# One transformer block on one core: V packed by pairs of tiles, value copies moved, norm work of qkv dealt to other slots

## The chip, the cores and the metric

One NeuronCore of a Trainium2 chip runs the program. The metric is device time in microseconds (us) of one execution, median of several runs; lower is better. The engines are TensorE (PE, with its weight loads shown apart as PEld), VectorE (DVE), ScalarE (ACT), GpSimd (POOL) and SyncE (SP, which issues the transfers). Each works through its own list of instructions in order, and semaphores tie the lists together.

## The reference

Input x is (2, 1024, 288), the condition (2, 288). First a conditional rotation, then one transformer block with 16 heads of 18:

```python
U, _ = jnp.linalg.qr(P)                      # 288 x 64
R = _rotation(cond, W, b)                    # expm of a skew matrix, 64 x 64
z = jnp.einsum('btn,nd->btd', x, U)
z_rot = jnp.einsum('btd,bde->bte', z, R)
x = x + jnp.einsum('btd,nd->btn', z_rot - z, U)
# block: ada = silu(c) @ ada_w + ada_b, split in shift, scale, gate (msa, mlp)
x = x + gate_msa * _attention(_modulate(_layernorm(x), shift_msa, scale_msa), ...)
x = x + gate_mlp * _mlp(_modulate(_layernorm(x), shift_mlp, scale_mlp), ...)
```

Attention is not over the sequence but inside each token: `attn = einsum('nthd,ntkd->nthk', q * scale, k)`, a 16 x 16 matrix of heads by heads for every token, softmax over k, then times v. The weights are large, so the kernel carries most operands as a high and a low float16 part.

## The kernel before

The 2048 tokens are 16 tiles (NT) of 128, in 4 chunks (NCH) of TPC = 4 tiles. A prologue computes the basis, the matrix exponential and the modulation (0 to 110 us). Then come qkv (120 to 207 us), attention (212 to 275 us), projection and the MLP.

**qkv.** It runs over slots `gu`. A unit (n, i, a, w) is one tile of chunk n and one of q, k, v (w = 0, 1, 2); twelve units (NQ) make a chunk. In each slot every engine goes through its own loop, written out by hand:
- TensorE: `turn` (a transpose block of the next chunk's normalised tokens) at the slots in TURN_AT, `qkv(gu)` (L819, seven matmuls of 288 columns; it waits for `low(gu - 2)`, since there are two banks UB), then the `job`s of the slot (L803 for q and k, L781 in `v_columns` for V: transposes of the finished q, k, v of a pair of tiles, two jobs a slot from slot 7), in some slots `maxima` (L768), and `delta` (L719, the rotation of a later tile) at the slots in DELTA_AT.
- ScalarE: `turn_out` (L1082, two results for each block of a turn), `high(gu)` (L1099, L1094: the float16 high part of a unit), `norm_root` (L1057, the square root for the layer norm of chunk 1 at slot 1, of chunk n + 2 at slot 8 of chunk n), and `job_out` (L1115, L1113: a cast of each job).
- VectorE: `split` (L1372, low part of a turn), `low(gu)` (L1418), `rotated` (L1384) and `stat` (L1318, L1320: statistics of a tile), `norm_var` (L1326), `norm_scales` (L1334 to L1342, five steps on 4 values a partition), `source` (L1351, normalises one tile an instruction, then L1356), and `maximum` (L1377).
- GpSimd: from the third unit on it folds the gate into the projection weights (L511 to L523).

The V half of a pair of tiles lies in HV as (slot, head, high/low, 18), with the two tiles (c_) in slots of their own. `v_columns` transposes each (head, tile) to 36 rows of a bank, tile 0 at partition 0 and tile 1 at partition 64 (R); `job_out` casts partitions 0 to 99 to VT. `v_groups` multiplies 36-row pieces of VT by SELV, which adds high and low part and puts tokens back on the partitions: bank VB[c_] holds tile c_, 16 groups of 18. `v_out` (L1150) copies both banks to VG for the values.

**Attention.** It is a loop over steps st. TensorE: `scores(st)` (L858), `maxima` of later steps, `values(st - 1)` (L895), late V transposes (`v_late`, L781, V of the second batch, four calls in steps 0 and 1 of each group of four from step 12), `turn_values` (L911) at step 2 of a group, `v_groups` (L881) at step 3. ScalarE: `exponentials` (L1141), `v_out`, and `values_out` (L1158), which copies four steps' values out of PSUM, up to step 16; from step DVE_AT = 17 VectorE does that copy (L1471), at steps 20, 24, 28, 32. VectorE also has `v_late_out` (L1475) and `normalise` (L1460, L1462). From step 11 on two pairs of score banks are used in turn (PAIRED = 10).

## Time and profile before

| | |
|---|---|
| time, median of 3 runs | 417.76 us (417.73 to 418.84) |
| the profiled execution | 418.09 us, of which the span from first to last instruction is 416.4 |
| busy: TensorE, its weight loads | 391.4 us (94%), 253.8 (61%) |
| busy: VectorE, ScalarE, GpSimd | 272.4 (65%), 228.0 (55%), 118.4 (28%) |
| granted TensorE clock, mean | 0.992 of full |
| chain that ended last | PE 72%, DVE 12%, ACT 10%, issue 6% |

The page names lines, engines and tiles; "L781 PE" is an instruction that line 781 issues on TensorE. Busy time of TensorE counts a matmul until its result has left the array, so neighbours overlap and a sum of durations is more than the time that they take. "Idle" times in square brackets tell how long the engine stood idle before a piece and what released it.

### The profile page before, as it was taken

The numbers are of one execution on the slowest core, as the hardware profiler recorded it, in microseconds if no ns is written. First come the engines' busy times: TensorE is split into PE (matmuls) and PEld (weight loads), VectorE is DVE, ScalarE is ACT, GpSimd is POOL, SyncE is SP. The second block draws the span as 40 slices with busy tenths as digits, with TensorE's granted clock in tenths as the row PEclk, the third lists the DMA queues.
The fourth block names the chain that finished last, engine by engine and source line by source line (L and its number), as shares of the span: only waits on it lengthen the run. The fifth ranks groups of instructions, "written<-read, shape, count | busy, mean of one in ns | idle before, by whom it ended". The sixth has DMA issues, their size and how long they took to land.

```text
span 416.4 us, 11776 instructions
## 1 busy us (share of the span) xinstructions
PE 391.4 (94%) x4799; PEld 253.8 (61%) x4799; DVE 272.4 (65%) x779; ACT 228.0 (55%) x478; POOL 118.4 (28%) x141
## 2 busy tenths in 40 slices
PE   8999999999988899999989788889999999999996
PEld 4665465666545566667656566568655575656575
DVE  2688885677689846655536256666899776756452
ACT  3356444432255799999876866656775432332200
POOL 6029999973009600010000000006500010101040
PEclk9999999999999999999979999999999999999999
DMA  5999100020000000000000000000000000000011
GB/s 163 298 318 270 50 4 2 2 74 2 2 0 2 2 2 3 2 3 6 2 6 6 3 3 3 2 3 2 1 2 1 16 28 16 30 14 30 14 45 43
DMA packets 8223, 15.30 MB, mean 37 GB/s; under 512 B 2591, under 2 KB 6279, under 8 KB 8044
## 3 DMA queue, kind: packets, MB, share of 16 engines
q1 hardware_dynamic: 8170, 14.56, 11.6%
q8 instruction: 38, 0.62, 0.6%
q14 instruction: 15, 0.12, 0.1%
HBM read 12.11 MB, written 2.38 MB: 35 GB/s over the span
## 4 chain that ended last, share of the span: by engine, by line
PE 72%; DVE 12%; ACT 10%; issue 6%; ACTq 0%; DVEq 0%
PE psum L972 13%; PE psum L988 13%; PE psum L541 9%; PE psum L819 5%; ACT scratch L1082 3%; PE psum L803 3%; PE psum L895 3%; ACT big L1115 3%; PE psum L633 2%; PE psum L949 2%; PE psum L645 2%; PE psum L597 2%; PE psum L624 2%; PE psum L911 2%; PE psum L637 1%
## 5 line engine op out<-in xcount | busy, mean ns | idle before, releaser
L972 PE MATMUL psum<-scratch,W 128*128 128x512 f16 (+1 forms) x252 | 57.9, 379 | 0.0
L988 PE MATMUL psum<-W,big 128*128 128x288 f16 x432 | 55.1, 286 | 0.0
L819 PE MATMUL psum<-WQ,scratch 128*128 128x288 f16 (+1 forms) x336 | 49.2, 287 | 4.5 <-DVE stage L1418 1.9
L1203 ACT ACTIVATE big<-psum 128x512 f32<-128x512 f32 x36 | 21.3, 597 | 57.3 <-PE psum L972 52.3
L988 PEld LDWEIGHTS psum<-W,big 128*128 128x128 f16 x432 | 42.2, 98 | 12.9
L541 PE MATMUL psum<-ident 128*32 128x192 f32 (+3 forms) x146 | 44.1, 386 | 0.0
L530 POOL TENSOR_TENSOR X<-X,big 128x288 f32<-128x288 f32 x16 | 13.0, 825 | 107.7 <-ACT big L1178 107.3
L1141 ACT ACTIVATE big<-psum 128x1024 f32<-128x1024 f32 x32 | 32.9, 1031 | 16.6 <-PE psum L858 16.3
L972 PEld LDWEIGHTS psum<-scratch,W 128*128 128x128 f16 (+1 forms) x252 | 24.7, 98 | 25.6
L819 PEld LDWEIGHTS psum<-WQ,scratch 128*128 128x128 f16 (+1 forms) x336 | 29.9, 98 | 15.4 <-DVE stage L1418 2.9
L1082 ACT ACTIVATE scratch<-psum,MOD 128x512 f32<-128x512 f32 (+3 forms) x48 | 34.4, 775 | 5.9 <-PE psum L744 4.6
L535 POOL TENSOR_TENSOR X<-X,scratch 128x288 f32<-128x288 f32 x16 | 13.5, 855 | 83.6 <-DVE big L1528 83.6
L1115 ACT CAST big<-psum 128x512 f16<-128x512 f32 x64 | 34.5, 599 | 0.1
L1041 ACT ACTIVATE scratch<-psum,scratch 64x65 f32<-64x65 f32 x63 | 19.5, 309 | 26.6 <-DVE scratch L1275 26.6
L1526 DVE TENSOR_SCALAR big<-big 128x512 f16<-128x512 f32 x36 | 15.6, 434 | 26.9 <-ACT big L1203 26.8
L1528 DVE SCALAR_TENSOR_TENSOR big<-big 128x512 f16<-128x512 f32 x36 | 26.3, 732 | 1.2
L1038 ACT ACTIVATE scratch<-scratch 64x1 f32<-64x1 f32 x63 | 12.8, 202 | 25.3 <-DVE scratch L1270 24.7
L1377 DVE TENSOR_REDUCE MX<-psum 128x16 f32<-128x1024 f32 x16 | 19.5, 1218 | 9.9 <-PE psum L768 9.9
L895 PE MATMUL psum<-big,scratch 128*32 128x128 f32 x512 | 23.1, 292 | 2.7 <-ACT scratch L1158 1.4
L1372 DVE TENSOR_TENSOR scratch<-scratch 128x512 f16<-128x512 f32 (+1 forms) x24 | 17.8, 740 | 11.3 <-ACT scratch L1082 11.1
L1099 ACT ACTIVATE stage<-psum 128x576 f16<-128x576 f32 x32 | 21.0, 655 | 7.0 <-PE psum L819 6.4
L803 PE MATMUL psum<-ident,stage 128*64 128x128 f16 x512 | 22.4, 223 | 2.4 <-ACT big L1115 1.4
(219 smaller groups left out, 758.3 us busy)
## 6 DMA issues: line engine op xcount, KB each, us to landing
X<-in_x_dram SPq DMA_DIRECT2D x4, 576.0 KB, 15.9
out_dram<-big SPq DMA_DIRECT2D x16, 144.0 KB, 1.7
big<-in_L_cond_W_dram SPq DMA_DIRECT2D x1, 2268.0 KB
big<-in_L_cond_ada_w_dram SPq DMA_DIRECT2D x2, 864.0 KB, 18.7
stage<-in_L_cond_fc_w_dram SPq DMA_DIRECT2D x1, 1296.0 KB, 19.4
big<-in_L_cond_fc_w_dram SPq DMA_DIRECT2D x1, 1152.0 KB
stage<-in_L_cond_qkv_w_dram SPq DMA_DIRECT2D x1, 864.0 KB
big<-in_L_cond_fc_w_dram SPq DMA_DIRECT2D x3, 144.0 KB
```

What stands on the lines that cost most here:

```text
L541: pe.matmul(out[:, 0:cols], left, left[:, 0:1].broadcast_to([P, cols]), start=True, stop=True)
L803: mm = pe.matmul(out[R * c_:R * c_ + R, P * hh:P * hh + P], HQ[:, 2 * (pr % 2) + c_, w, 4 * q + hh, :], ident16[:, :], start=True, stop=True)
L819: mm = pe.matmul(UB[gu % 2][:, 0:D], HT[0:r, n % 2, a_, P * a:P * a + P], WQ[0:r, w_, D * w:D * w + D], start=(p_ == 0), stop=(p_ == 6))
L895: mm = pe.matmul(PO[c_][32 * g:32 * g + 32, P * q:P * q + P], VG[:, w % 2, c_, 4 * q + g, :], E[:, s_ % 2, c_, P * g:P * g + P], start=Tru ...
L972: mm = pe.matmul(FB[idx % 3], W1[0:r, w_, P * m:P * m + P], HT[0:r, n % 2, a_, :], start=(p_ == 0), stop=(p_ == 6))
L988: mm = pe.matmul(YB[t % 2][:, 0:D], g[:, a_, f, cols], W2[:, w_, f, :], start=(f == 0 and a_ + w_ == 0), stop=(f == NF - 1 and w_ == 1))
L1082: act.activation(dst, src, ACT.Identity, scale=MOD[0:rows, 2 * l + 1, b, batch:batch + 1], bias=MOD[0:rows, 2 * l, b, batch:batch + 1]).th ...
L1099: act.mul(dst[:, :, 0:2, :] if w else dst[:, :, 0:3:2, :], src.unsqueeze(2).broadcast_to([P, H, 2, DH]), QSCALE / (FINE * FINE)).then_inc( ...
L1115: act.copy(columns(QKT[pr // 4][:, w, :], 16 * (pr % 4), q), src.rearrange("p (h v m) -> p h v m", h=4, v=32)).then_inc(col_done, 1)
L1141: act.activation(E[:, s_ % 2, :, :], psum[:, 3:5, :] if s_ > PAIRED and s_ % 2 else psum[:, 0:2, :], ACT.Exp, scale=DH ** -0.5 / (QSCALE * ...
L1203: act.activation(G32[:, idx % 2, :], FB[idx % 3], ACT.Gelu, scale=1.0 / (FINE * FINE)).then_inc(gelu_sb, 1)
L1528: dve.scalar_tensor_tensor(out=GT[c_ % 2][:, 1, m, :], in0=G32[:, idx % 2, :], scalar=FINE, in1=GT[c_ % 2][:, 0, m, :], op0=ALU.mult, op1= ...
```

## The change

- HV holds the two tiles of a pair side by side: (slot of pair, head, tile, high/low, 18). `v_columns` issues one matmul a head with 72 weight columns, where it issued two of 36; the result is 72 rows from partition 0. The casts on ScalarE and VectorE take partitions 0 to 71 instead of 0 to 99.
- SELV is 72 x 36 and its setup has two steps instead of four. `v_groups` issues 16 matmuls with 72 rows and 36 columns instead of 32 with 36 rows and 18 columns; a bank now holds 8 groups of both tiles, and `v_out` permutes while it copies.
- DVE_AT goes from 17 to 9: the value copies at steps 12 and 16 are VectorE's.
- In chunk 0 of qkv the turn for chunk 1 goes from slots 5, 6, 7 to 6, 8, 10 and the deltas from 4 to 7 to 5 to 8. On VectorE the last two statistics of chunk 1 are split over slots 0 and 1 (the first waits for one rotated tile less), `norm_var(1)` comes in slot 1, behind `low(1)`, `norm_scales(1)` goes from slot 1 to 3, its `source` from slots 2, 3 to 4, 5; ScalarE's `norm_root(1)` from slot 1 to 2.
- For chunks 2 and 3 `norm_root` goes from slot 8 to 9 of the chunk two before, `norm_scales` from 9 to 10; `source` stays at 10 and 11.

```diff
@@ -132,7 +132,7 @@
         BN = sb("BN", [P, 2, 6])
-        SELV = sb("SELV", [P, DH], F16)
+        SELV = sb("SELV", [P, 2 * DH], F16)
         ident16 = sb("ident16", [P, P], F16)
@@ -149,7 +149,7 @@
         o += 5 * CH
-        HV = scratch[:, o:o + 8 * D].bitcast(F16).rearrange("p (a h s d) -> p a h s d", a=8, h=H, s=2)
+        HV = scratch[:, o:o + 8 * D].bitcast(F16).rearrange("p (a h c s d) -> p a h c s d", a=4, h=H, c=2, s=2)
         assert o + 8 * D <= 4 * 2112 + 2 * D
@@ -269,8 +269,8 @@
         TURN1_AT = {2 * NCH: (3, 5, 7), 2 * NCH + 1: (5, 7, 8), 2 * NCH + 2: (3, 5, 7)}
-        TURN_AT = ((5, 6, 7), (2, 4, 6), (2, 4, 6), ())
-        DELTA_AT = ((4, 5, 6, 7), (1, 3, 5, 7))
+        TURN_AT = ((6, 8, 10), (2, 4, 6), (2, 4, 6), ())
+        DELTA_AT = ((5, 6, 7, 8), (1, 3, 5, 7))
         FC2_AT = (2, 4, 6, 8)
@@ -313,7 +313,7 @@
         PAIRED = 10
-        DVE_AT = 17
+        DVE_AT = 9
         EXP_TABLE_AT = 3 * NQ - 1
@@ -460,9 +460,9 @@
-            chain(pool.tensor_copy(SELV[:, :], ident[:, 0:DH]))
-            for j in (DH, R, R + DH):
-                chain(pool.tensor_tensor(SELV[:, :], SELV[:, :], ident[:, j:j + DH], ALU.add))
+            for c_ in range(2):
+                at = 2 * DH * c_
+                chain(pool.tensor_tensor(SELV[:, DH * c_:DH * c_ + DH], ident[:, at:at + DH], ident[:, at + DH:at + 2 * DH], ALU.add))
@@ -775,12 +775,10 @@
-                slot = 4 * (pr // 2 % 2) + 2 * (pr % 2)
                 for hh in range(4):
-                    for c_ in range(2):
-                        mm = pe.matmul(out[R * c_:R * c_ + 2 * DH, P * hh:P * hh + P],
-                                       HV[:, slot + c_, 4 * q + hh, :, :].rearrange("p s d -> p (s d)"), ident16[:, :],
-                                       start=True, stop=True)
+                    mm = pe.matmul(out[0:4 * DH, P * hh:P * hh + P],
+                                   HV[:, 2 * (pr // 2 % 2) + pr % 2, 4 * q + hh].rearrange("p c s d -> p (c s d)"), ident16[:, :],
+                                   start=True, stop=True)
                 return mm
@@ -875,11 +873,8 @@
                 for g in range(16):
-                    for c_ in range(2):
-                        r = R * c_
-                        at = P * (16 * (w % 4) + g)
-                        mm = pe.matmul(VB[c_][:, DH * g:DH * g + DH], VT[r:r + 2 * DH, at:at + P], SELV[r:r + 2 * DH, :],
-                                       start=True, stop=True)
+                    at, to = P * (16 * (w % 4) + g), 2 * DH * (g % 8)
+                    mm = pe.matmul(VB[g // 8][:, to:to + 2 * DH], VT[0:4 * DH, at:at + P], SELV[0:4 * DH, :], start=True, stop=True)
                 mm.then_inc(vg_psum, 1)
@@ -1091,7 +1086,7 @@
                         act.wait_ge(col_ready, JOB[(2 * (n - 2) + i // 2, 2, 3)] + 1)
-                    act.mul(HV[:, 4 * (n % 2) + i, :, 0, :], src, QSCALE / (FINE * FINE)).then_inc(qk_high, 1)
+                    act.mul(HV[:, 2 * (n % 2) + i // 2, :, i % 2, 0, :], src, QSCALE / (FINE * FINE)).then_inc(qk_high, 1)
                     return
@@ -1110,7 +1105,7 @@
                 if w == 2:
-                    act.copy(columns(VT, 16 * pr, q)[0:R + 2 * DH], src[0:R + 2 * DH, :].rearrange("p (h v m) -> p h v m", h=4, v=32)).then_inc(col_done, 1)
+                    act.copy(columns(VT, 16 * pr, q)[0:4 * DH], src[0:4 * DH, :].rearrange("p (h v m) -> p h v m", h=4, v=32)).then_inc(col_done, 1)
                 else:
@@ -1125,11 +1120,11 @@
                     high(gu)
-                if gu == 1:
+                if gu == 2:
                     norm_root(1)
                 for i in slots.get(gu, ()):
                     job_out(i)
-                if m == 2 * TPC and n + 2 < NCH:
+                if m == 2 * TPC + 1 and n + 2 < NCH:
                     norm_root(n + 2)
@@ -1146,8 +1141,9 @@
                     act.wait_ge(pv_ready, 4 * w - 4)
-                for c_ in range(2):
-                    cp = act.mul(VG[:, w % 2, c_, :, 0:DH], VB[c_][:, 0:16 * DH].rearrange("p (g d) -> p g d", g=16), 1.0 / QSCALE)
+                for v in range(2):
+                    cp = act.mul(VG[:, w % 2, :, 8 * v:8 * v + 8, 0:DH],
+                                 VB[v][:, 0:16 * DH].rearrange("p (g c d) -> p c g d", g=8, c=2), 1.0 / QSCALE)
                 cp.then_inc(vg_ready, 1)
@@ -1411,7 +1407,7 @@
                 if w == 2:
-                    hi, lo = HV[:, 4 * (n % 2) + i, :, 0, :], HV[:, 4 * (n % 2) + i, :, 1, :]
+                    hi, lo = HV[:, 2 * (n % 2) + i // 2, :, i % 2, 0, :], HV[:, 2 * (n % 2) + i // 2, :, i % 2, 1, :]
                 else:
@@ -1425,14 +1421,16 @@
                 if gu == 0:
+                    dve.wait_ge(x_rot, 2 * TPC - 1)
+                    stat(0, TPC + 2)
+                if gu == 1:
                     dve.wait_ge(x_rot, 2 * TPC)
-                    stat(0, TPC + 2)
                     stat(0, TPC + 3)
                     norm_var(1)
-                if gu == 1:
+                if gu == 3:
                     norm_scales(1)
-                if gu in (2, 3):
-                    source(1, 0, (range(0, 2), range(2, 4))[gu - 2])
+                if gu in (4, 5):
+                    source(1, 0, (range(0, 2), range(2, 4))[gu - 4])
                 if gu in AHEAD:
@@ -1440,7 +1438,7 @@
                         norm_var(n + 2)
-                    if m == 2 * TPC + 1:
+                    if m == 2 * TPC + 2:
                         norm_scales(n + 2)
@@ -1472,8 +1470,8 @@
                 dve.wait_ge(vcol_ready, 4 * (w - 4) + q + 1)
-                dve.tensor_copy(columns(VT, 16 * (w - 4), q)[0:R + 2 * DH],
-                                VB[q % 2][0:R + 2 * DH, :].rearrange("p (h v m) -> p h v m", h=4, v=32)).then_inc(vcol_done, 1)
+                dve.tensor_copy(columns(VT, 16 * (w - 4), q)[0:4 * DH],
+                                VB[q % 2][0:4 * DH, :].rearrange("p (h v m) -> p h v m", h=4, v=32)).then_inc(vcol_done, 1)
             for st in range(UNITS + 3):
                 for s_ in later(st):
```

## Rows read from the trace of the kernel before

**Rows 1.** The page, busy time, share of the span and instructions of TensorE
```profile
PE 391.4 (94%) x4799; PEld 253.8 (61%) x4799; DVE 272.4 (65%) x779; ACT 228.0 (55%) x478; POOL 118.4 (28%) x141
```

**Rows 2.** Busy time by stretch: us, PE, PEld, DVE, ACT, POOL busy; clock; DMA
```profile
120.00:144.20 24.20, 18.95 (x189) 11.94 (x190) 21.63 (x56) 15.31 (x30) 17.00 (x18) 1.00 0.00 1
144.20:167.30 23.10, 22.45 (x303) 15.18 (x302) 13.53 (x39) 22.05 (x44) 0.00 (x0) 1.00 0.01 3
...
212.30:220.30 8.00, 7.23 (x234) 5.11 (x236) 4.48 (x4) 4.53 (x6) 0.00 (x0) 0.57 0.03 7
...
235.60:243.40 7.80, 6.58 (x168) 4.56 (x168) 3.92 (x8) 5.56 (x9) 0.00 (x0) 1.00 0.01 2
```

**Rows 3.** Groups by line, TensorE: the V transposes; busy us, mean ns, idle before
```profile
L781 PE MATMUL psum<-ident,scratch 128*36 128x128 f16 x256 | 10.7, 221 | 1.5 <-DVE big L1475 0.9 <-ACT big L1115 0.4
```

**Rows 4.** The chain of waits in qkv: start us, us held, what
```profile
148.48 1.40 ACT scratch L1082 x2
...
154.25 0.54 ACT stage L1099
154.79 0.97 ACT big L1115 x2
...
165.83 0.97 PE psum L819 x7
166.80 0.56 PE psum L781 x16
...
197.54 1.83 PE psum L819 x14
```

**Rows 5.** Timeline of TensorE at step 11 of attention: start us, us, instruction
```profile
235.63 0.56 PE L881 MATMUL psum<-SELV,big 36*128 36x18 f16 x32 [0.25 <-DVE stage L1462]
236.03 0.40 PE L858 MATMUL psum<-big 63*128 63x128 f16 x8
236.36 0.64 PE L895 MATMUL psum<-big,scratch 128*32 128x128 f32 x16
```

**Rows 6.** Timeline of ScalarE: the V copies that close four groups of steps
```profile
236.22 0.72 ACT L1150 ACTIVATE scratch<-psum 128x288 f32<-128x288 f32 x2 [0.36 <-PE psum L881]
...
244.04 0.72 ACT L1150 ACTIVATE scratch<-psum 128x288 f32<-128x288 f32 x2 [0.36 <-PE psum L881]
...
251.85 0.71 ACT L1150 ACTIVATE scratch<-psum 128x288 f32<-128x288 f32 x2 [0.36 <-PE psum L881]
...
259.52 0.72 ACT L1150 ACTIVATE scratch<-psum 128x288 f32<-128x288 f32 x2 [0.35 <-PE psum L881]
```

**Rows 7.** Timeline of VectorE: norm steps and scalings in chunk 0 of qkv
```profile
124.03 0.17 DVE L1326 TENSOR_SCALAR ST<-MV 128x4 f32<-128x4 f32 x1
...
124.68 0.91 DVE L1336 TENSOR_TENSOR ST<-ST 128x4 f32<-128x4 f32 x1
...
126.95 1.72 DVE L1351 TENSOR_SCALAR scratch<-X,MV,ST 128x288 f32<-128x288 f32 x2
...
140.09 0.43 DVE L1326 TENSOR_SCALAR ST<-MV 128x4 f32<-128x4 f32 x1
```

**Rows 8.** Timeline of GpSimd: three of its 18 operations between 124.17 and 142.4
```profile
124.17 1.40 POOL L511 TENSOR_TENSOR big<-big 128x576 f32<-128x576 f32 x1 [13.59 <-PE psum L819]
...
126.40 1.28 POOL L513 TENSOR_TENSOR WP<-big,WP 128x576 f16<-128x576 f32 x1
...
131.14 1.41 POOL L511 TENSOR_TENSOR big<-big 128x576 f32<-128x576 f32 x1
```

**Rows 9.** Timeline of TensorE: the starts of units 4, 6 and 12
```profile
127.09 1.03 PE L819 MATMUL psum<-WQ,scratch 128*128 128x288 f16 x7 [1.45 <-DVE scratch L1418]
...
132.04 1.02 PE L819 MATMUL psum<-WQ,scratch 128*128 128x288 f16 x7
...
144.19 1.03 PE L819 MATMUL psum<-WQ,scratch 128*128 128x288 f16 x7
```

**Rows 10.** Who waited for whom, ScalarE, 120 to 144.2 us: in total, times, longest
```profile
ACT ST L1057 <- DVE ST L1326: 3.1, 2, 2.1
```

## The prediction

> **What bounds the kernel now.** The page comes first: TensorE is busy for 94% of the span [rows 1]. That share counts the pipeline's tail, so it doesn't say that TensorE sets every stage; the busy time in stretches does [rows 2]. In 120.0 to 144.2 us, where the first twelve units of qkv run, TensorE works 18.95 of 24.2 us, ScalarE 15.31, VectorE 21.63: nobody is full, the three wait for one another, and it is the one stretch of qkv that leaks. In 144.2 to 167.3 TensorE is at 97% and ScalarE at 95%, so a gain on one of them alone is mostly lost to the other. In attention (from 212.3) four score steps form a loop with a fixed period; in 235.6 to 243.4 TensorE has 6.58 of 7.8 us to do. The edits touch these three places and nothing else; prologue, projection and MLP stay.
>
> **Packed V: the transposes.** `v_columns` issues 256 matmuls of 128 columns in 32 calls of 8, 10.7 us of busy time [rows 3]. After, there are 128, each with 72 weight columns instead of 36. Counted by the mean that would be half. But look at the price of a column: in the chain of waits 7 qkv matmuls (288 columns, whole array) hold it for 0.97 us and 14 for 1.83 [rows 4], so 7 more cost 0.86, 0.123 each, 0.43 ns a column; one matmul of 128 columns alone costs 0.055. Sixteen transposes hold the chain for 0.56 us [rows 4], 0.035 each, which is less than a single one costs: the two of a pair run side by side in two column halves. Four packed ones cost what four pairs cost, 0.22 us. Nothing is saved here.
>
> What does change is what lies beside them. Seven qkv matmuls need 7 x 0.123 = 0.86 us, and hold the chain for 0.97 where transposes follow. Eight pairs need 0.44, and hold it for 0.56. So each change of the array's shape costs about 0.1 us. In the new form the transposes have the shape of qkv (72 columns don't fit a half), and both changes go. In qkv eight slots hold V jobs, hence 8 entries and 5 exits to a whole-array shape (four to qkv, one to a turn): at most 1.3 us. It counts only where TensorE is the later one. Two of the four slot pairs stand beside a turn, where ScalarE is behind; at the other two it idles 0.2 to 0.3 us a slot, so about 0.2 of each slot comes through. I take -0.4, ends 0 and -1.3. In attention the late transposes stand between the values (32 columns) and the row-tiled scores: both changes stay, 0.
>
> The Trainium skill, "TensorEngine Tiling (Array Packing)", Key Properties, says that changing the tiling mode drains the array; by that rule too the whole-array neighbours save a drain, and the rows agree. Its section The Solution promises up to 2x for sides of 64 or less when two tiles run at once, which speaks against fusing two tiles into one.
>
> **Packed V: the group sums.** `v_groups` issues 32 matmuls of 36 rows and 18 columns a call, in two row halves: from 235.63 to the scores at 236.03 it is 0.40 us, 0.025 for a pair [rows 5]. After: 16 of 72 rows and 36 columns on the whole array. By the column rate 36 columns are 0.015 us, under the present 0.025, so I keep 0.40. No row shows a 128-column weight load on the whole array with so short a matmul behind it; the bound above is that a matmul as wide as its load costs 0.055, so 16 would be 0.88, +0.48 us a call; the bound below is 0 (a call already pays 0.025 for a pair of loads). I take 0, the row nearest in shape. But the exit is new. Before, sums and scores have the same shape and follow with no gap, whereas from scores to values it is 0.33 us [rows 5] for 4 pairs at 0.055: 0.1 for the change of shape. That 0.1 now stands between sums and scores too. In the first three groups ScalarE hides it: its V copy of 0.72 [rows 6] lies ahead of the next exponential. From step 11 on, once VectorE owns the value copies, the loop is values, copy, late V copies, turn, normalise, sums, scores, values, and it lies on the path: 5 x 0.1 = +0.5.
>
> **Values by VectorE from unit 9.** The copies at steps 12 and 16 move. On ScalarE they lie between two exponentials. From V copy to V copy such a group takes 244.04 - 236.22 = 7.82 us; with the copy on VectorE 259.52 - 251.85 = 7.67 [rows 6]. Both kinds hold the same late V work, so the move is worth 2 x 0.15 = -0.3. VectorE has the room (3.92 of 7.8 us [rows 2]). Queued behind the copy on it are the late V copies, and the next turn waits for those; that wait is inside the 7.67. Attention together: +0.2, ends -0.3 and +0.7.
>
> **The norm work dealt anew.** This is the hard part, since GpSimd folds the projection weights from 124.17 on almost without a pause, and VectorE's operations from SBUF to SBUF wait for its current one. A step on 4 values took 0.17 us at 124.03, before GpSimd's start, and 0.91 at 124.68, ending at 125.59 with GpSimd's operation of 124.17 to 125.57; two row scalings took 1.72 [rows 7, 8]. Unblocked, two take 0.8. The Trainium skill, "SBUF — State Buffer", section "SBUF: two separate sides", says that the shared port pair is an exclusive lock held for a whole instruction; these ends agree.
>
> Before: the variance of chunk 1 is taken 0.14 us ahead of GpSimd's start; the scales follow at once, and unit 2's low half waits behind them, so that unit 4 starts at 127.09 [rows 9]. The scalings run from 126.95 [rows 7] to 129.9, then the first turn, unit 5 and a second turn; unit 6 starts at 132.04 [rows 9]. After, on VectorE:
> - low(1) goes ahead of the last statistics (0.6 us): unit 3 starts 0.7 earlier, at 123.9. The variance then falls at 124.4, inside GpSimd's first operation, and is held to 125.6, as the one at 140.09 took 0.43 [rows 7]. low(2) stands behind it: unit 4 at 126.05, 1.0 earlier.
> - The scales come after low(3), from 126.9. Two or three of their four lockable steps meet GpSimd's operations up to 129.0: they end at 128.5 to 129.05, and low(4) waits behind them.
> - Four scalings with low(5) between, each behind what GpSimd holds: the last one ends at 131.2 to 132.6. The first turn ends and unit 6 starts at 131.8 to 132.9. But before, a second turn (0.49) and one more delta (0.47) were done by unit 6.
> - From there ScalarE has three turns (1.40 each), five high halves (0.54), eight casts (0.97 a pair) [rows 4] and the root (0.2): 11.0 us, from about 132.3. Its longest wait for a root, 2.1 us [rows 10], shrinks to about 0.5, since that root is asked for a slot later, behind unit 9's casts. Unit 12's start follows the last of these casts by 0.3.
> Unit 12 comes out at 144.0 to 145.3 against 144.19 [rows 9]; I take 144.6, +0.4. With no port conflict the same chain puts the first turn at 129.4 and unit 12 at about 141.5.
> In chunk 1's turn for chunk 3 scales and scaling share a slot, 1.0 + 0.8 us ahead of the next low half, which the two qkv banks cover (TensorE has a slot of 1.5 us and the maxima in hand). 0, and +0.5 if that cover is gone. The SELV setup on GpSimd is two steps shorter, long before use: 0.
>
> **The sum.** Against the profiled execution (418.09 us: 416.4 of span and 1.7 around it): -0.4 for changes of shape, +0.2 for attention, +0.4 for the norm work: +0.2, 418.3. The median of the runs shown (417.76) is 0.33 lower: 418.0.
>
> **Rivals.**
> 1. The norm work wins: the steps slip through GpSimd's gaps, and ScalarE's 3.1 us of waits for roots [rows 10] vanish. Unit 12 at 141.5 to 143, -1.2 to -2.7; with the rest 414.9 to 416.4. For it: low(1) and low(2) are plainly freed. Against it: GpSimd's gaps are under 0.1 us. Chance 0.2.
> 2. Slower by the lock: the last scaling misses its gap and waits for GpSimd's 1.41 us from 131.14 [rows 8], the first split waits for the next one, the second root is late once more: unit 12 at 145.5 or later, +1.3 to +2, and no slack to bring in the changes of shape: 419.2 to 420. It decides from the point where the last scaling starts after 131.14. Chance 0.13.
> 3. Weight loads bound the group sums: +0.48 in seven calls on the path, +3.4: 421.4. Chance 0.05. The Trainium skill, "TensorE: Matmul & The Clock Gate", section "Weight-path perf modes", says that a load of 128 columns in 16 bits is fast whatever its rows, which speaks against it.
> 4. Halving by count: half of 10.7 us [rows 3], -5.3: 412.5. The side by side pairs stand against it. Chance 0.02.
> 5. The clock: around 212.3 to 220.3 it was 0.57 [rows 2], half speed for most of the group. It took 8.0 us without a turn of the values (1.1 us of TensorE), the later ones 7.8 with one, so the dip costs about 1.1. If the shifted work removes it: 416.9; a second dip: 419.1. Chance 0.05 each way.
>
> **How the numbers follow.** The likeliest (0.5, ends 416.9 to 419.0) gives 418.0. A measurement tells 0.3% (1.25 us) from no change: faster is under 416.5, slower over 419.0. Faster: most of rival 1, rival 4 and an edge of 5: 0.22. Slower: rivals 2 and 3: 0.18. Same: 0.60. The range takes in the near parts of rivals 1 and 2: 415.9 to 419.6.
>
> **What would show it.** Right: 128 transposes, four in what four pairs took; qkv before them holds the chain for 0.86 instead of 0.97; sums 0.40 us and scores 0.1 later; the group from step 12 at 7.75; the variance of chunk 1 at over 1 us instead of 0.17; the wait for the second root under 1 us; unit 12 at 144.6. Wrong: a variance that isn't held, a first turn before 130.5, sums over 0.5 us, or groups still at 7.8.

## The result and the profile after

Forecast was 418.0 us, 415.9 to 419.6, most likely no change. The changed kernel took 421.86 us in the median of 9 runs, against 418.33 for the kernel before on the same chip. Some executions of nearly every kernel fall into a slower state (here four of the nine, 432.8 to 436.8 us, and one of the nine before); ratios and the medians given from here on leave them out (421.31 against 418.15), and as the profiled executions of e1, e6, e7, e10, e11 and e13 are of that kind, with a prologue 12 to 49 us longer, their units are told from the start of unit 0 and their whole spans are not compared. The ratio is 1.0058, 95% interval 1.0033 to 1.0083: slower by 0.6%, about 2.4 us, and the time lies over the range's upper end. The profiled execution was 421.86 us with a span of 420.0, against 418.09 and 416.4, so the two traces differ by 3.6 us, and these 3.6 us are to be found. (The four other executions that count took 419.89 to 421.32, so the trace shows the longest of them.)

Line numbers moved up by two to five: qkv is L817, its turns' first transposes L744, V transposes L779, group sums L877, scores L856; on VectorE the low halves are L1414, variance L1322, scales L1330 to L1338, scalings L1347; on ScalarE roots are L1052.

Busy time by stretch in the changed kernel (columns as in [rows 2]):
```profile
120.00:144.20 24.20, 18.89 (x149) 11.45 (x149) 19.53 (x44) 12.36 (x23) 16.30 (x18) 0.86 0.00 1
...
238.85:246.60 7.75, 6.85 (x136) 4.70 (x137) 5.08 (x10) 4.71 (x7) 0.00 (x0) 1.00 0.01 2
```
The first row is the main finding. In the same 24.2 us TensorE was busy as long as before (18.89 against 18.95 us, [rows 2]) but got through 149 matmuls instead of 189, at a granted clock of 0.86 instead of 1.00. A busy share alone would have hidden it: the count beside it and the clock column show that the engine worked slower, not longer. The attention group, the last row, has 136 instructions where there were 168.

The starts answer to [rows 9]. TensorE in the changed kernel, from unit 2 to unit 12 of qkv:
```profile
123.07 1.96 PE L817 MATMUL psum<-WQ,scratch 128*128 128x288 f16 x14 [0.38 <-DVE stage L1414]
126.17 1.94 PE L817 MATMUL psum<-WQ,scratch 128*128 128x288 f16 x14 [1.15 <-DVE scratch L1414]
...
130.06 0.67 PE L744 MATMUL psum<-order,scratch 128*128 128x128 f32 x2 [1.48 <-DVE scratch L1347]
131.22 0.33 PE L744 MATMUL psum<-order,scratch 128*128 128x128 f32 x1 [0.49 <-DVE scratch L1347]
132.70 0.47 PE L744 MATMUL psum<-order,scratch 128*128 128x128 f32 x1 [1.15 <-DVE scratch L1347]
132.97 1.89 PE L817 MATMUL psum<-WQ,scratch 128*128 128x288 f16 x7
...
135.62 1.86 PE L817 MATMUL psum<-WQ,scratch 128*128 128x288 f16 x7
...
139.41 1.02 PE L817 MATMUL psum<-WQ,scratch 128*128 128x288 f16 x7
...
147.87 0.41 PE L817 MATMUL psum<-WQ,scratch 128*128 128x288 f16 x2
```
(The last row is cut by the view's end; unit 12 has its seven too.) Unit 6 starts at 132.97, unit 12 at 147.87, against 132.04 and 144.19. Units 6 and 7 take 1.89 and 1.86 us for the seven matmuls that take 1.02 before and after them. VectorE over the same stretch, to be read beside [rows 7]:
```profile
124.55 1.21 DVE L1322 TENSOR_SCALAR ST<-MV 128x4 f32<-128x4 f32 x1
...
127.14 0.69 DVE L1332 TENSOR_TENSOR ST<-ST 128x4 f32<-128x4 f32 x1
127.87 0.71 DVE L1334 TENSOR_TENSOR ST<-ST 128x4 f32<-128x4 f32 x1
...
129.49 0.86 DVE L1347 TENSOR_SCALAR scratch<-X,MV,ST 128x288 f32<-128x288 f32 x2
130.28 0.44 DVE L1414 SCALAR_TENSOR_TENSOR scratch<-psum,scratch 128x288 f16<-128x288 f32 x1
130.64 2.01 DVE L1347 TENSOR_SCALAR scratch<-X,MV,ST 128x288 f32<-128x288 f32 x2
```
and GpSimd's operations that these meet, as in [rows 8]:
```profile
124.33 1.40 POOL L511 TENSOR_TENSOR big<-big 128x576 f32<-128x576 f32 x1 [13.60 <-PE psum L817]
...
131.08 1.40 POOL L511 TENSOR_TENSOR big<-big 128x576 f32<-128x576 f32 x1
```
The variance of four values takes 1.21 us and ends with GpSimd's operation (125.73); the last pair of scalings takes 2.01 and ends at 132.65, behind the one that ends at 132.48. And the clock around that, from windows of the changed kernel:
```profile
128.60:132.70 4.10, 0.96 (x4) 0.42 (x4) 3.98 (x9) 0.00 (x0) 3.74 (x5) 0.88 0.02 4
131.70:138.50 6.80, 5.80 (x35) 3.21 (x36) 4.68 (x9) 3.08 (x5) 6.30 (x8) 0.50 0.00 0
220.50:223.90 3.40, 3.40 (x86) 2.34 (x82) 2.44 (x2) 1.05 (x2) 0.00 (x0) 0.50 0.02 5
```
In 4.1 us ahead of unit 6 TensorE worked 0.96: three transposes, and a fourth at 132.70 that unit 6 waits for. The clock fell at 131.7, inside this gap, to 0.50 (1.2 instead of 2.4 GHz), and stayed there for 6.8 us. Before, the dip stood in attention (213.3 to 220.1, [rows 2]); a shorter one is left there.

### The profile page after: what moved, and what is told of

It reads as the page before. It is cut to its first block, busy times and chain, and to the rows that moved or that the text cites. A ratio compares the mean times of both kernels' runs of the same rounds, so it can differ in the third digit from the quotient of the medians.

```text
span 420.0 us, 11263 instructions
## 1 busy us (share of the span) xinstructions
PE 393.2 (94%) x4543; PEld 255.6 (61%) x4543; DVE 275.5 (66%) x783; ACT 226.3 (54%) x474; POOL 117.1 (28%) x139
## 4 chain that ended last, share of the span: by engine, by line
PE 73%; DVE 11%; ACT 10%; issue 5%; POOL 1%; ACTq 0%; DVEq 0%
PE psum L967 13%; PE psum L983 13%; PE psum L541 8%; PE psum L817 5%; ACT scratch L1077 3%; PE psum L944 3%; PE psum L801 3%; PE psum L890 3%; ACT big L1110 3%; PE psum L633 2%; PE psum L645 2%; PE psum L597 2%; PE psum L624 2%; DVE scratch L1469 2%; PE psum L906 2%
## 5 line engine op out<-in xcount | busy, mean ns | idle before, releaser
L817 PE MATMUL psum<-WQ,scratch 128*128 128x288 f16 (+1 forms) x336 | 50.6, 294 | 2.5 <-DVE scratch L1414 1.2
L541 PE MATMUL psum<-ident 128*32 128x192 f32 (+3 forms) x146 | 44.1, 386 | 0.0
L817 PEld LDWEIGHTS psum<-WQ,scratch 128*128 128x128 f16 (+1 forms) x336 | 30.6, 100 | 14.0 <-DVE scratch L1414 1.7
## 6 DMA issues: line engine op xcount, KB each, us to landing
out_dram<-big SPq DMA_DIRECT2D x16, 144.0 KB, 1.7
big<-in_L_cond_fc_w_dram SPq DMA_DIRECT2D x3, 144.0 KB
```

The costliest lines, as they stand in the source:

```text
L541: pe.matmul(out[:, 0:cols], left, left[:, 0:1].broadcast_to([P, cols]), start=True, stop=True)
L817: mm = pe.matmul(UB[gu % 2][:, 0:D], HT[0:r, n % 2, a_, P * a:P * a + P], WQ[0:r, w_, D * w:D * w + D], start=(p_ == 0), stop=(p_ == 6))
```

## The experiments

Two theories at the start. **A**: the norm work loses by the port conflict with GpSimd's folding, and half clock follows. **B**: the loss comes from packed V or from the order of the norm work in itself. First each part alone.

**e1_pack and e11_pack_again: packed V alone** on the kernel before, with all hunks on `SELV`, `HV`, `VG` and the 72-row copies; the core of it:
```diff
-                    for c_ in range(2):
-                        mm = pe.matmul(out[R * c_:R * c_ + 2 * DH, P * hh:P * hh + P],
+                    mm = pe.matmul(out[0:4 * DH, P * hh:P * hh + P],
...
-                    for c_ in range(2):
-                        r = R * c_
+                    at, to = P * (16 * (w % 4) + g), 2 * DH * (g % 8)
```

> Only the packed V on top of the kernel before. My theory: it saves nothing by itself; changes of shape gain 0.1 to 0.4 us in qkv, and 0.1 us between group sums and scores costs up to 0.5 us in attention. Sum 417.5 to 418.5 against about 418.0 before, group period on VectorE's copies 7.74 instead of 7.67, unit 12 still at 144.2 us. Rival (the packing is what made the changed kernel slower): 420 or more.

> The packed V alone on the kernel before, once more, for a second profile and a tighter interval than 0.9948 to 1.0006. Theory (the two changes of array shape around each slot's V transposes go, sums to scores gains 0.09 us, and nothing else): 416.9 to 418.0, groups of four attention steps at 7.81 us with the values on ScalarE and 7.74 with them on VectorE, unit 12 within 0.3 us of +24.13. Rival (the gaps inside the bursts of small matmuls early in attention go too, since half as many instructions are issued): attention's first four groups together over 0.5 us shorter than in the kernel before, 416 to 417.

Measured: 0.9977 (0.9948 to 1.0006), and 0.9993 (0.9969 to 1.0016) the second time: no change that can be told. Relative to unit 0, unit 12 stands at +24.00 in e11 against +24.13. Its V copies, in attention:
```profile
255.97 0.71 ACT L1145 ACTIVATE scratch<-psum 128x288 f32<-128x288 f32 x2 [0.35 <-PE psum L877]
263.78 0.72 ACT L1145 ACTIVATE scratch<-psum 128x288 f32<-128x288 f32 x2 [0.35 <-PE psum L877]
271.52 0.72 ACT L1145 ACTIVATE scratch<-psum 128x288 f32<-128x288 f32 x2 [0.35 <-PE psum L877]
```
7.81 us with the values on ScalarE, 7.74 with them on VectorE, where [rows 6] has 7.82 and 7.67: the new shape change between sums and scores costs 0.07 where VectorE owns the values and nothing where ScalarE does. Its first attention group took 6.90 us with no half clock in it, against 8.00 in the kernel before with 6.8 us of half clock, so such a stretch costs 1.1 us there, as priced. e3, which is not packed and has no half clock in attention either, took 6.89, so packing has no part in that. The rival of the second text stays open. By its letter it came true, since the first four groups together are 1.0 us shorter than before; but the first group's clock makes all of that, and the next two take 8.00 and 7.45 us, against 7.90 and 7.45 in the kernel before, whose trace has no gap inside a burst of values.

e1's own trace shows something else: half clock for 6.8 us in chunk 0, from 8.7 us behind the start of unit 0, though the norm work is in its old order. Unit 6 came at +13.72 and unit 12 at +24.93, where e11, the same kernel, has +11.97 and +24.00.

**e2_dve: the values alone.**
```diff
-        DVE_AT = 17
+        DVE_AT = 9
```


> Only the value copies of steps 12 and 16 on VectorE. My theory: two groups go from 7.82 to 7.67 us, -0.3 us in all. Rival (VectorE's queue puts the late V copies behind and delays the turn): both groups at 8 us or more, +0.4 us.

Measured: 0.9993 (0.9975 to 1.0011), span 415.9. ScalarE's V copies in e2:
```profile
235.75 0.71 ACT L1150 ACTIVATE scratch<-psum 128x288 f32<-128x288 f32 x2 [0.35 <-PE psum L881]
243.43 0.71 ACT L1150 ACTIVATE scratch<-psum 128x288 f32<-128x288 f32 x2 [0.35 <-PE psum L881]
```
Both moved groups take 7.68 (the second ends at 251.10) instead of 7.82: -0.3 together, the forecast's term.

Its trace too has half clock in chunk 0, with the old order: 3.4 us from 127.2 on, where the 4.1 us ahead hold 1.98 us of work.
```profile
120.00:144.20 24.20, 20.07 (x191) 12.51 (x189) 21.49 (x55) 15.30 (x30) 16.98 (x18) 0.93 0.00 1
```
```profile
126.78 1.45 PE L819 MATMUL psum<-WQ,scratch 128*128 128x288 f16 x7 [1.45 <-DVE scratch L1418]
...
143.85 1.03 PE L819 MATMUL psum<-WQ,scratch 128*128 128x288 f16 x7
```
Unit 6 is 0.5 us late, but unit 12 starts at +24.10 from unit 0 (119.75), no later than before. So half clock in chunk 0 is not the new order's alone, and its price hangs on where it falls: nothing here, 0.9 us in e1, about 3 in the changed kernel (e9 below).

**e3_norm: the norm work alone**, with the hunk of e4 and the split of the statistics that e13 undoes (both below), chunk 1's root, scales and scalings in their new slots, and
```diff
-        TURN_AT = ((5, 6, 7), (2, 4, 6), (2, 4, 6), ())
-        DELTA_AT = ((4, 5, 6, 7), (1, 3, 5, 7))
+        TURN_AT = ((6, 8, 10), (2, 4, 6), (2, 4, 6), ())
+        DELTA_AT = ((5, 6, 7, 8), (1, 3, 5, 7))
```

> Only the norm work dealt anew. My theory: all of the loss is here, +2 to +3.7 us over the kernel before (420 to 421.7): the first turn ends after 132.5 us, TensorE idles over 3 us before it and its clock falls to half for 6.8 us there; unit 12 at 146.5 to 148 us. Rival (the loss needs the packing too): under 419.5.

Measured: 1.0060 (1.0031 to 1.0089), span 420.0, the changed kernel's ratio and span. Unit 6 starts at 132.89, unit 12 at 147.88. Windows of e3 ahead of unit 6 and behind it:
```profile
128.50:132.60 4.10, 0.97 (x4) 0.42 (x3) 3.96 (x9) 0.00 (x0) 3.71 (x5) 0.88 0.01 4
131.60:138.40 6.80, 5.78 (x35) 3.19 (x36) 4.67 (x9) 3.06 (x5) 6.31 (x8) 0.50 0.00 0
```
The whole loss, with its gap and its dip, is the norm work's: packed V (0.9977 and 0.9993) and the values (0.9993) show none of it alone.

**e4_roots: of that, only the later roots and scales of chunks 2 and 3.**
```diff
-                if m == 2 * TPC and n + 2 < NCH:
+                if m == 2 * TPC + 1 and n + 2 < NCH:
                     norm_root(n + 2)
...
-                    if m == 2 * TPC + 1:
+                    if m == 2 * TPC + 2:
                         norm_scales(n + 2)
```


> Of the norm work only the second part: root and scales of chunks 2 and 3 one slot later, chunk 1 as before. My theory: ScalarE's wait of 2.1 us for the root at 138.4 to 140.6 us shrinks to under 1 us and unit 12 starts 0.3 to 1.3 us earlier than 144.2: 416.7 to 417.7. Rival (scales and scaling in one slot put the next low half late): 418 or more, unit 12 or 13 not earlier.

Measured: 1.0003 (0.9979 to 1.0026). Unit 12 starts at 143.14, 0.9 earlier from unit 0 than before, and the first scores 1.0 earlier (210.53). But attention's first two groups give it back: 8.12 and 8.66 us instead of 8.00 and 7.90. TensorE in the second of them:
```profile
223.01 0.64 PE L895 MATMUL psum<-big,scratch 128*32 128x128 f32 x14 [0.19 <-issue]
...
227.71 0.42 PE L895 MATMUL psum<-big,scratch 128*32 128x128 f32 x7 [0.46 <-issue]
```
The gaps lie inside a burst of values whose operands are there, and the profile names no releaser. The traces of e3, e10 and e12, not packed either, have one such gap each, 0.42, 0.17 and 0.46 us; those of the kernel before, of e2 and of the packed kernels have none. What makes them stays open, and whether packing removes them too. The time, 417.88 in the median, shows no gain, though the forecast was 416.7 to 417.7.

**e5_fold_late: the changed kernel, folding later.** The one-line edit starts GpSimd's folding behind unit 14 instead of unit 2.
```diff
-            pool.wait_ge(qk_ready, 3)
+            pool.wait_ge(qk_ready, 15)
```


> The changed kernel, with GpSimd's folding of the projection weights started after unit 14 instead of unit 2, so that nothing holds VectorE in chunk 0. Theory A (the port makes the turn late): variance of chunk 1 back at 0.17 us, first turn ends at 129 to 130 us, no half clock there, unit 12 at 141.5 to 143 us instead of 147.9; the run 415 to 418 us, so 3 us or more of the loss is gone. Theory B (the new order itself is late, whatever GpSimd does): unit 12 at 146 us or later, 420 or more.

Measured: 0.9946 (0.9926 to 0.9966), a median of 416.56 us, where the changed kernel has 1.0058: 1.1%, or nearly 5 us, less. VectorE, the same steps as above:
```profile
125.48 0.17 DVE L1322 TENSOR_SCALAR ST<-MV 128x4 f32<-128x4 f32 x1
...
127.25 0.16 DVE L1332 TENSOR_TENSOR ST<-ST 128x4 f32<-128x4 f32 x1
...
129.46 0.76 DVE L1347 TENSOR_SCALAR scratch<-X,MV,ST 128x288 f32<-128x288 f32 x2
```
0.17 instead of 1.21, 0.16 instead of 0.69, 0.76 instead of 2.01. Unit 6 stands at +9.29 from unit 0 (121.15) instead of +12.75, unit 12 at +21.11 instead of +27.65, with the clock at 1.00. Theory A stands: without the lock there is neither the late turn nor the half clock. Attention took two half-clock stretches of 3.4 us each.

**e6_warm and e9_warm8: the gap filled.** The changed kernel with 12, then 8, calls into an idle bank ahead of chunk 1's first turn, two instructions each; what they compute is read by nobody.
```diff
+                        if gu == 6:
+                            for _ in range(8):
+                                clock(CB[0], ident[:, :], 2 * P)
```


> The changed kernel with 12 idle matmuls (0.32 us each, 3.8 us) on TensorE ahead of chunk 1's first turn, into a bank that nobody uses yet. The wait for the turn stays, only the clock can differ. Theory A1 (the half clock behind the wait costs about 2.5 us of the 3.6): no half clock at 131 to 139 us, unit 6 still at 132.9, unit 12 at 145 to 145.5 instead of 147.9, 418 to 419.5 us. Theory A2 (the wait alone is the loss, the clock costs under 0.5 us): unit 12 at 147.4 or later, 420.5 or more.

> The changed kernel with 8 extra matmuls into an idle bank on TensorE, in the gap ahead of chunk 1's first turn (12 in the run before, where they overshot the gap by about 1.3 us). At full clock 8 take about 1.7 us, at half clock 3.4. Theory (TensorE's idle stretch of about 4.3 us costs the clock, and the half clock costs 3.0 us between units 6 and 12): unit 6 stays at about +12.75 us from unit 0's start, no half clock follows it, and unit 12 comes at +24.6 to +25.2 instead of +27.65; the time is 418.3 to 419.5, that is 2 to 3 us under the changed kernel. If the busy stretch is too short and the clock falls all the same, unit 12 stays at +27.6 and the time at 421 to 422. Rival (the loss sits in the order, not in the clock): unit 12 at +27 or later whatever the clock does, 421 or more.

Measured, e6: 1.0043 (1.0018 to 1.0067), a median of 419.68 us, just over the forecast; 12 were too many, unit 6 came 1.3 us late, at +14.06, but with the clock at 1.00 it took 11.89 us from unit 6 to 12 instead of 14.90. e9: 1.0042 (0.9999 to 1.0084); of the seven times that the comparison rests on five are 417.3 to 418.64 and two 422.42 and 423.51, hence the wide interval. No trace shows what those two met. Its profiled execution is one of the five, with a span of 416.8:
```profile
120.00:144.20 24.20, 21.48 (x193) 14.60 (x194) 20.65 (x50) 14.96 (x29) 16.35 (x18) 1.00 0.01 1
131.70:138.50 6.80, 6.69 (x73) 4.28 (x72) 5.82 (x13) 5.43 (x10) 6.31 (x8) 1.00 0.00 0
212.90:219.80 6.90, 6.11 (x193) 4.36 (x196) 3.74 (x4) 3.62 (x6) 0.00 (x0) 0.51 0.02 6
```
```profile
128.20 3.75 PE L541 MATMUL psum<-ident 128*128 128x256 f32 x16
...
132.56 1.02 PE L817 MATMUL psum<-WQ,scratch 128*128 128x288 f16 x7
...
144.38 1.02 PE L817 MATMUL psum<-WQ,scratch 128*128 128x288 f16 x7
```
The idle work (L541; 3.75 us at full clock, not the 1.7 expected) fills the gap, the clock stays at 1.00 through 131.7 to 138.5, where 73 instructions pass instead of 35. Nothing on VectorE or GpSimd changed; the last scalings still take 2.01 us. Unit 12 stands at +24.47 from unit 0 (119.91): 3.2 us less than the +27.65 of the changed kernel, and 0.3 more than the kernel before. So of the 3.5 us by which unit 12 is late, 3.2 are clock and 0.3 all the rest, the later turn among it. In the time the same holds only for those five executions.

**e7_pack_dve_roots and e8_pdr_fold: the change without chunk 1's new slots**, then with the line of e5 too. Against the changed kernel e7 has the statistics of e13 (below) and
```diff
-        TURN_AT = ((6, 8, 10), (2, 4, 6), (2, 4, 6), ())
-        DELTA_AT = ((5, 6, 7, 8), (1, 3, 5, 7))
+        TURN_AT = ((5, 6, 7), (2, 4, 6), (2, 4, 6), ())
+        DELTA_AT = ((4, 5, 6, 7), (1, 3, 5, 7))
...
-                if gu == 2:
+                if gu == 1:
                     norm_root(1)
...
-                if gu == 3:
+                if gu == 1:
                     norm_scales(1)
-                if gu in (4, 5):
-                    source(1, 0, (range(0, 2), range(2, 4))[gu - 4])
+                if gu in (2, 3):
+                    source(1, 0, (range(0, 2), range(2, 4))[gu - 2])
```

> The changed kernel with chunk 1's norm work, turn and deltas put back to their old slots; packing, value copies, and the later roots of chunks 2 and 3 stay. If the parts add: roots -0.9 us at unit 12, packing -0.5 to -1.0, copies -0.3: 416 to 417 us. If the gains are given back in the first two groups of attention (as with the roots alone): 417.5 to 418.5. No gaps of 0.4 us or more inside TensorE's bursts in 211 to 236 us, where the unpacked kernels have them at full clock.

> As the one with chunk 1's work put back, and GpSimd's folding started after unit 14. Theory A: chunk 0's steps are no longer held (0.91 back to 0.2, 1.72 back to 0.8), first turn ends at about 128.5 instead of 130.1 us, unit 12 at 141 to 142 us: 414.5 to 416 us, unless the folding now holds VectorE and with it ScalarE in 147 to 165 us, which would give 1 us or more back (unit 24 no earlier than 166).

Measured, e7: 0.9979 (0.9955 to 1.0002), unit 12 at +23.15, 0.85 us earlier than in e11. Its first two groups of attention took 7.88 and 7.97 us, so they don't give the gain back as in e4, and there is no gap inside a burst, as expected. Yet the ratio can't be told from those of packed V alone, so the roots' gain isn't shown in the time. e8: 0.9926 (0.9903 to 0.9949), 415.17 us, unit 12 at +19.81. Against e5, which has chunk 1's new slots and no conflict either, that is 1.3 us earlier: at unit 12 the new order of chunk 1's norm work is worse also with no lock in it. (The two ratios' intervals overlap.)

**e12_fold_only: the kernel before with the folding late.**
```diff
-            pool.wait_ge(qk_ready, 3)
+            pool.wait_ge(qk_ready, 15)
```

> The kernel before with GpSimd's weight folding started after unit 14 instead of unit 2, and nothing else. Theory (the port conflict is what chunk 0 of qkv leaks): unit 6 at +9.5 to +10.5 us from unit 0 instead of +11.98, unit 12 at +20.5 to +21.5 instead of +24.13, and 415 to 416.5, some of the 3 us given back early in attention; and then packed V, VectorE's values and the later roots are worth 0.3 to 1.3 us more (the kernel with all four took 415.18). Rival (the gain of 3 us came mainly from the later roots and packed V, with late folding only helping them): unit 12 at +22.5 or later and 417 or more.

Measured: 0.9912 (0.9890 to 0.9935), a median of 414.13 us from only three executions, and a span of 412.7. Starts of units 0 and 12 on TensorE (a query that ended at 140.9 cuts the second):
```profile
120.45 0.91 PE L819 MATMUL psum<-WQ,scratch 128*128 128x288 f16 x6 [0.53 <-DVE scratch L1372]
...
140.75 0.42 PE L819 MATMUL psum<-WQ,scratch 128*128 128x288 f16 x2
```
Unit 12 at +20.30 instead of +24.13. And the folding costs nothing where it went; e12's stretch of units 12 to 24:
```profile
140.70:163.80 23.10, 22.46 (x306) 15.17 (x300) 14.75 (x37) 22.05 (x45) 16.52 (x18) 1.00 0.01 3
```
It is the row 144.20:167.30 of [rows 2] with 16.5 us of GpSimd added: as long, TensorE 22.46 against 22.45, ScalarE the same; VectorE's busy time grew by the 1.2 us in which it was held, and it has 8 us to spare.

**e10_split_rows: the kernel before with the two statistics split**, the second one and the variance behind low(1).
```diff
                 if gu == 0:
+                    dve.wait_ge(x_rot, 2 * TPC - 1)
+                    stat(0, TPC + 2)
+                if gu == 1:
                     dve.wait_ge(x_rot, 2 * TPC)
-                    stat(0, TPC + 2)
                     stat(0, TPC + 3)
                     norm_var(1)
-                if gu == 1:
                     norm_scales(1)
```


> The kernel before with one thing moved on VectorE: of chunk 1's two last statistics, the second, with the variance behind it, goes behind low(1); square root, scales, scalings, turns and deltas stay in the kernel before's slots. Theory (the variance of 4 values now falls inside GpSimd's first folding step and is held about 1.2 us; what the early low half gains is paid back by that lock): unit 3 about 0.6 us earlier, the variance 1.0 to 1.25 us instead of 0.17, the first turn and unit 6 0.3 to 1.5 us later than the kernel before, unit 12 at +24.1 to +25.6 from unit 0 (24.13 before); 418 to 419.8. Rival (the late root and scales of chunk 1 are what costs, not the variance): unit 12 at or under +24.1 and 417.5 to 418.3.

Measured: 1.0079 (1.0049 to 1.0109). In e10 VectorE has
```profile
137.82 1.21 DVE L1326 TENSOR_SCALAR ST<-MV 128x4 f32<-128x4 f32 x1
...
139.97 1.13 DVE L1340 TENSOR_SCALAR ST<-ST 128x4 f32<-128x4 f32 x1
```
and TensorE
```profile
142.39 1.03 PE L819 MATMUL psum<-WQ,scratch 128*128 128x288 f16 x7 [4.11 <-DVE scratch L1418]
```
```profile
143.40:146.80 3.40, 3.40 (x15) 1.96 (x14) 3.37 (x6) 2.10 (x3) 3.09 (x5) 0.50 0.02 5
```
Held variance and held scales (the last of them 0.71 at 141.14) follow each other, low(2) waits behind both, TensorE stands still for 4.11 us, and at 143.4, 1.0 us after it has begun again, its clock falls to half for 3.4 us. Unit 6 is at +14.36, unit 12 at +25.33. The theory was right in kind, and its median, 420.93 us, lies over the forecast's 419.8. The size was underrated (unit 6 was to be 0.3 to 1.5 us late and is 2.4).

**e13_var_early: the changed kernel with that split undone**, everything else of the change kept. It asks which move makes the changed kernel's gap: the late variance, or the later scales and scalings.
```diff
                 if gu == 0:
-                    dve.wait_ge(x_rot, 2 * TPC - 1)
+                    dve.wait_ge(x_rot, 2 * TPC)
                     stat(0, TPC + 2)
-                if gu == 1:
-                    dve.wait_ge(x_rot, 2 * TPC)
                     stat(0, TPC + 3)
                     norm_var(1)
```

> The changed kernel with chunk 1's two last statistics and its variance ahead of low(1) again, as in the kernel before; root, scales, scalings, turns and deltas of chunk 1 stay in their new slots. [...] Rival (the later scales and scalings make the gap): the last scaling stays behind the operation that ends at about 132.5, the gap stays near 4 us, the half clock comes, unit 12 at +27 or later, 420.5 to 422.

Measured: 1.0088 (1.0054 to 1.0122) from three executions, with a median of 422.47: the rival, no gain. The profiled execution had a mean granted clock of 0.66, so its TensorE is not compared; VectorE's steps are:
```profile
172.41 0.17 DVE L1322 TENSOR_SCALAR ST<-MV 128x4 f32<-128x4 f32 x1
...
175.73 0.75 DVE L1332 TENSOR_TENSOR ST<-ST 128x4 f32<-128x4 f32 x1
...
179.28 2.01 DVE L1347 TENSOR_SCALAR scratch<-X,MV,ST 128x288 f32<-128x288 f32 x2
```
The variance is free again at 0.17, and the last scalings still take 2.01. So what is left of the new order (root, scales, scalings, turns and deltas in later slots; no run parts these) suffices for the loss, and by e10 the split with its late variance suffices without it. That the gap ahead of the first turn was again near 4 us in e13's other executions is concluded from its times, not seen.

**e14_pd_fold: e8 without the later roots**, that is with the hunks of e4 undone.
```diff
-                if m == 2 * TPC + 1 and n + 2 < NCH:
+                if m == 2 * TPC and n + 2 < NCH:
...
-                    if m == 2 * TPC + 2:
+                    if m == 2 * TPC + 1:
                         norm_scales(n + 2)
```

> The kernel before with packed V, VectorE's values from unit 9 and the late folding, and without any move of the norm work. Theory (the roots of chunks 2 and 3 cost only where the folding holds VectorE, so later ones are worth under 0.5 us here): unit 12 at +20.0 to +20.6 from unit 0 against +20.30 with late folding alone and +19.81 with the later roots, and 413.9 to 415. Which way it falls in that hangs on whether attention's third group meets a half clock (1.3 us). Rival (the later roots keep their 1 us gain): unit 12 at +20.8 or later, 415.2 to 416.

Measured: 0.9912 (0.9891 to 0.9933), 414.13 us, unit 12 at +20.20 against +19.81 with them. The theory holds: they are worth 0.4 us at unit 12, and in the time nothing that shows. e8, e12 and e14 can't be told apart: all are 0.7 to 0.9% under the kernel before, and what they share is the late folding. So e12's theory failed in its second half: packed V, the values and the later roots (e8) add nothing to it that shows.

## Why the prediction was wrong, point by point

- **The step that failed** is the last of the norm work: "Unit 12 comes out at 144.0 to 145.3". It took what ScalarE has to do from unit 6 on (11.0 us) at the pace that the trace of before shows, with TensorE at full clock. The trace showed the other pace, in the dip of [rows 2] that rival 5 names, but that rival was placed at attention only. (The terms named there, 132.3 + 11.0 + 0.5 + 0.3, come to 144.1; the 144.6 that was taken has 0.5 us that no term names.) The chain that led to unit 6 was sized well: last scaling forecast to end at 131.2 to 132.6, measured 132.65; unit 6 at 131.8 to 132.9, measured 132.97, both just past the late end. What wasn't drawn from it is what stood between: with deltas and second turn gone from the stretch, TensorE has 0.96 us of work in 4.1, and its clock is at half for 6.8 us. Units 6 to 12 took 14.90 us instead of the 11.82 at full clock in e9. With the gap filled so, unit 12 started at 144.38 and five of seven times were 417.3 to 418.6, where 144.6 and 418.0 had been forecast for the kernel itself. In the trace the clock is the whole miss.
- The Trainium skill, "TensorE: Matmul & The Clock Gate", section "Why this matters for your kernels", warns of idle gaps between bursts in the middle of a kernel because the clock falls back. The traces agree (e10: half clock after 4.11 us of standstill); e3 and the changed kernel add that the clock fell with three transposes in the gap, and e2 that it can fall where the longest standstill ahead was 1.45 us.
- **Rival 2** named the mechanism (the last scaling misses its gap and waits for GpSimd's operation from 131.14) and came true at 131.08. Its price was wrong on both sides: unit 12 at 145.5 or later for the lock alone, where e9 shows +0.3 us, and nothing for the clock. Its chance of 0.13 was too low for a mechanism that the likeliest case had inside its own range of 131.2 to 132.6.
- **The lock on VectorE**: right. The variance "over 1 us instead of 0.17" is 1.21, two or three of the four lockable scales were to be held, two were (0.69 and 0.71), and a third by 0.1 (0.26). The Trainium skill's exclusive lock ("SBUF — State Buffer", "SBUF: two separate sides") agrees: with the folding late all of them fall to 0.16 or 0.17.
- **With no port conflict** unit 12 was put at 141.5. e5 has it at 142.26, or +21.1 from unit 0, and 141.5 is +21.4 from 120.06: right.
- **The second root's wait**: forecast under 1 us, measured 0.44, against 2.1 in [rows 10]. Right, and in the time no gain shows: e4 and e14.
- **Changes of shape**: right in kind. Qkv before the V transposes now holds the chain of waits for 0.86 instead of 0.97, and 8 transposes for 0.45:
```profile
148.03 0.86 PE psum L817 x7
148.89 0.45 PE psum L779 x8
```
  The term was -0.4. From unit 12 to the first scores it is 67.20 us instead of 67.34; in e11, from unit 0 to the first scores, 91.10 instead of 91.46. So 0.1 to 0.4 us.
- **Packed V does not halve**: right. Four packed transposes take what four pairs took, the sums don't grow (rival 3 fell: 16 of them at 0.025 each are 0.40 us; that its 421.4 is close to the measured time is chance), the scores follow 0.49 after the sums instead of 0.40. (The "up to 2x" that the prediction takes from the Trainium skill, "TensorEngine Tiling (Array Packing)", stands there under "Theoretical Speedup".) TensorE in the changed kernel:
```profile
238.88 0.55 PE L877 MATMUL psum<-SELV,big 72*128 72x36 f16 x16 [0.25 <-DVE stage L1460]
239.37 0.40 PE L856 MATMUL psum<-big 63*128 63x128 f16 x8
...
242.44 0.39 PE L779 MATMUL psum<-ident,scratch 128*72 128x128 f16 x4 [0.26 <-DVE big L1473]
```
- **Attention**: forecast groups of 7.75 from step 12 on, measured 7.74 (V copies of the changed kernel below). The sum of +0.2 came out near 0, since the drain costs 0.07 a group rather than 0.1 and the moved groups gain the rest.
```profile
239.47 0.71 ACT L1145 ACTIVATE scratch<-psum 128x288 f32<-128x288 f32 x2 [0.35 <-PE psum L877]
247.21 0.72 ACT L1145 ACTIVATE scratch<-psum 128x288 f32<-128x288 f32 x2 [0.35 <-PE psum L877]
```

## What to carry to other kernels

When an order by hand is changed, add up what TensorE still has to do between the moved steps: behind a stretch of about 4 us with under 1 us of work, half clock cost 3.2 us here, ten times what all the rest of the new order cost, and the trace of before already showed that the clock falls in this kernel. When two engines lock each other out, first move the one that nobody waits for to where the other has slack: one number in one wait (e12) gave 0.9%, while the rearrangement around the conflict lost 0.6%. And a gain upstream is a gain only once the next stage has been seen to keep it (e4's trace gave back 0.9 us of 1.0).

## What the runs showed of the hardware that was not expected

- TensorE's clock fell to 0.50 although the gap held transposes: 0.96 us of work in 4.1 (the changed kernel; 0.97 in e3). In e5 the stretch of the same steps (127.0 to 131.1) held 3.33 us of work and stayed at 1.00, and in the kernel before 124.5 to 128.6 held 2.54 and stayed at 1.00. But e2 and e1, with the kernel before's order, fell to 0.50 in chunk 0 behind 4.1 us that held 1.98 and 2.65. All three traces with a gap like the changed kernel's (its own, e3, e10) have half clock behind it; without such a gap it came in some executions and not in others.
- In attention half clock lasted 3.4 or 6.8 us at a time, and where it falls differs between kernels with the same work there (213.3 before, 220.5 after, 210.9 in e12, 210.7 and 227.7 in e8, nowhere in e3 and e11). It costs 1.1 us in the first group (6.8 us of it) and 1.3 in e8's third (8.74 us instead of 7.46 in e12, 3.4 us of it). That is as large as what most of the edits tried changed; why it starts there stays open.
- Not every operation of VectorE is held: in the changed kernel its reciprocal of four values took 0.17 us at 126.94, inside GpSimd's operation of 126.54 to 127.82, while the product behind it took 0.69.
- Gaps of 0.2 to 0.5 us inside bursts of 16 small matmuls whose operands are ready (e4, and one each in e3, e10 and e12), put down to issue by the profile.
- The clock column can read 1.00 where TensorE works at half pace: e11's first 20 us hold 68 matmuls at 1.00, the kernel before's 114 at 1.00. Count and clock have to be read together.
